# Collecting the experts' sums: the first batch added on VectorE, the second later and normalised on ScalarE, input halves taken from PSUM, the projection in two halves

## The reference

```
x = _layernorm(x + _L0_ffn_ref(x, ...), axis=-1)        # the experts' sums; x included
kva = x @ wkv_a                                        # 256 -> 64 + 64
ckv, k_pe = (kva[..., :LORA], kva[..., LORA:])
ckv = ckv * rsqrt(mean(ckv * ckv, -1) + EPS) * kv_norm_scale
k_pe = _rope(k_pe, cos, sin)
```

## Time and profile before

| | us |
|---|---|
| runs shown | 1349.69, 1347.46, 1347.89; median 1347.89 |
| the profiled execution | 1350.13, its span 1348.3 |
| TensorE busy | 1174.2 (87% of the span) |
| VectorE busy | 783.9 (58%) |
| ScalarE busy | 735.6 (55%) |
| GpSimd busy | 955.8 (71%) |
| collect phase, from its first load to the first attention instruction | 449.85 to 491.99 |

### The profile page before, as it was taken

One profiled execution on the slowest core, in us unless ns is written; L12 is line 12 of the kernel. 1 busy time (PEld: TensorE's weight loads), 2 busy tenths in 40 slices (PEclk: granted clock), 3 DMA queues, 4 the chain that ended last, 5 costly groups with the idle time before them and its releaser, 6 DMA issues. The chain is left out here.

```text
span 1348.3 us, 18919 instructions
## 1 busy us (share of the span) xinstructions
PE 1174.2 (87%) x5570; PEld 879.9 (65%) x5625; DVE 783.9 (58%) x1712; ACT 735.6 (55%) x1389; POOL 955.8 (71%) x700
## 2 busy tenths in 40 slices
PE   6982779999999248999999997869999999998797
PEld 4882645555555146777777775847777777777586
DVE  4478822222222375777777772857777777754566
ACT  3220223333333026888888887227888888885242
POOL 2023948888887546889988886648988899967454
PEclk9995879999999578999999999969999999998799
DMA  9439245555555600000000000000000000002001
GB/s 326 152 126 241 56 107 82 82 79 81 81 79 77 180 9 9 8 9 8 1 9 9 1 1 13 1 16 4 6 9 9 9 9 1 1 0 70 0 16 47
DMA packets 66512, 68.22 MB, mean 51 GB/s; under 512 B 15072, under 2 KB 59680, under 8 KB 66304
## 3 DMA queue, kind: packets, MB, share of 16 engines
q1 hardware_dynamic: 48336, 43.36, 10.9%
q0 software_dynamic: 15168, 20.72, 10.0%
q10 hardware_dynamic: 2928, 3.15, 0.7%
HBM read 46.10 MB, written 21.10 MB: 50 GB/s over the span
## 5 line engine op out<-in xcount | busy, mean ns | idle before, releaser
L1537 POOL TENSOR_TENSOR att_prob_lo<-att_prob,att_prob_hi 128x1024 fp32r<-128x1024 f32 (+1 forms) x160 | 348.2, 2181 | 78.6 <-ACT att_prob_hi L1460 78.4
L1360 PE MATMUL all_bank<-att_q_hl,sequence_k_hl 128*128 128x512 f32 (+1 forms) x960 | 259.0, 380 | 0.0
L1383 PE MATMUL all_bank<-att_prob_hi,sequence_v_hl 128*128 128x512 f32 (+1 forms) x640 | 188.8, 376 | 5.9 <-POOL att_prob_lo L1537 3.1
L1360 PEld LDWEIGHTS all_bank<-att_q_hl,sequence_k_hl 128*128 128x128 f32 x960 | 173.0, 192 | 28.9
L1343 PE MATMUL all_bank<-sequence_k_hl,att_q_hl 128*128 128x512 f32 (+3 forms) x384 | 171.2, 450 | 18.7 <-DVE att_peak L1585 11.7
L1453 ACT ACTIVATE att_prob<-all_bank 128x1024 f32<-128x1024 f32 (+1 forms) x160 | 149.9, 937 | 62.7 <-PE all_bank L1366 56.2
L1460 ACT CAST att_prob_hi<-att_prob 128x1024 fp32r<-128x1024 f32 (+1 forms) x160 | 154.2, 964 | 5.1
L917 PE MATMUL all_bank<-early_w_gu,moe_xgT 128*128 x316 | 148.8, 553 | 3.6 <-issue 2.5
L882 POOL DMA_INDIRECT sums<-moe_y,early_slot_far x79 | 125.4, 1588 | 36.4 <-issue 20.8
L1572 DVE TENSOR_TENSOR all_xT<-all_bank,sequence_cst_turned 32x512 f32<-32x512 f32 x128 | 88.7, 693 | 96.7 <-PE all_bank L1330 95.7
L1596 DVE RECIPROCAL att_rden<-att_den 128x128 f32<-128x128 f32 x124 | 116.3, 944 | 29.0 <-POOL late_oT L1532 29.0
(11 more groups left out here) (246 smaller groups left out, 2192.4 us busy)
## 6 DMA issues: line engine op xcount, KB each, us to landing
sequence_w_raw<-wqk_rows SPq DMA_DIRECT2D x16, 256.0 KB, 2.6
early_w_gu<-in_gate SPq DMA_DIRECT2D x16, 224.0 KB, 5.7
early_w_gu<-in_up SPq DMA_DIRECT2D x16, 224.0 KB, 5.8
early_w_down<-in_down SPq DMA_DIRECT2D x1, 3584.0 KB, 20.0
sums<-early_zero SPq DMA_DIRECT2D x18, 128.0 KB, 3.7
all_xT<-in_xT SPq DMA_DIRECT2D x4, 512.0 KB, 8.5
all_x_tok<-in_x SPq DMA_DIRECT2D x1, 2048.0 KB, 16.3
x_rows<-all_x_tok SPq DMA_DIRECT2D x4, 512.0 KB, 3.0
```

Source lines behind the costliest of these rows:

```text
L1360: nc.tensor.matmul(ps, k_hl[:, ks, j * P:(j + 1) * P], q_hl[n % 2][:, qs, :, i * BW + q0:(i + 1) * BW], start=g == 0, stop=False)
L1383: mm = nc.tensor.matmul(out, v_hl[:, vs, j, :], part[:, u % 3, half * WIDE:half * WIDE + 2 * w].rearrange("p (h m) -> p h m", h=2), start= ...
L1537: nc.gpsimd.tensor_tensor(prob_lo[:, u % 3, 0:w], prob[:, u % 2, 0:w], prob_hi[:, u % 3, 0:w].bitcast(F32), ALU.subtract).then_inc(lo_sb, 1)
```

## The change

GpSimd no longer adds groups 0 and 1; VectorE does, ahead of each group's statistics. GpSimd's adds of groups 2 and 3 wait until all of batch 0 is normalised. Groups 2 and 3 are normalised by ScalarE as Identity(rstd * z + shift), with shift = -mean * rstd made on GpSimd in two small instructions per group. The halves of batch 0's input are no longer made from `xT` in SBUF: ScalarE casts and VectorE subtracts each of the four PSUM banks that hold the transposed tiles (`x_high`, `x_low`), and TensorE may reuse a bank only after both. TensorE projects tiles 0 to 3 between its first two groups of transposes, tiles 4 to 7 behind the second, and puts `turn` ahead of the last group. On VectorE the query weights' halves, and the copies of the projection, move ahead of batch 1's statistics. In the output phase the copies of the projection are only called from another place, in the same order.

```diff
@@ -1068,9 +1068,9 @@
-    def project(self, pe):
+    def project(self, pe, tiles=range(QT)):
         pe.wait_ge(self.loaded, 32)
-        for t in range(QT):
+        for t in tiles:
...
     def highs(self, act):
         self.nc.scalar.copy(self.x_hl[:, 0], self.x_own).then_inc(self.x_sb, 1)
+        self.ones_high(act)
+
+    def ones_high(self, act):
         act.wait_ge(self.ones_sb, 1)
         self.nc.scalar.copy(self.v_hl[:, 0, :, LORA:P], self.ones[:]).then_inc(self.v_sb, 1)
 
@@ -1096,15 +1099,18 @@
             act.wait_ge(self.turn_mm, g + 1)
             self.nc.scalar.copy(self.k_hl[:, 0, g * WIDE:(g + 1) * WIDE], self.turn_ps[g]).then_inc(self.k_sb, 1)
 
+    def begin(self, dve):
+        self.step = Count(self.step_sb, dve)
+
+    def copy_raw(self, dve, g):
+        dve.wait_ge(self.raw_mm, g + 1)
+        self.nc.vector.tensor_copy(self.raw[:, g * self.GT:(g + 1) * self.GT, :],
+                                   self.raw_ps[g].rearrange("p (t n) -> p t n", n=P)).then_inc(self.raw_sb, 1)
+
     def finish_rows(self, dve):
-        v, step = self.nc.vector, Count(self.step_sb, dve)
-        self.step = step
+        v, step = self.nc.vector, self.step
         half = ROPE // 2
         raw, rows = self.raw, self.rows
-        for g in range(self.G):
-            dve.wait_ge(self.raw_mm, g + 1)
-            v.tensor_copy(raw[:, g * self.GT:(g + 1) * self.GT, :], self.raw_ps[g].rearrange("p (t n) -> p t n", n=P)
-                          ).then_inc(self.raw_sb, 1)
...
             @block.gpsimd
             def _(pool):
-                for g in range(G):
+                def add(g):
                     at = slice(g * GT, (g + 1) * GT)
                     pool.wait_ge(loaded[g], 32)
                     nc.gpsimd.tensor_tensor(z[:, at, :], z[:, at, :], odd[:, at, :], ALU.add).then_inc(z_sb, 1)
-                    if g:
-                        norm.deviations(pool, g - 1)
-                norm.deviations(pool, G - 1)
+
+                def shifts(g):
+                    at = slice(g * GT, (g + 1) * GT)
+                    nc.gpsimd.tensor_scalar(less_mean[:, at], norm.meanvar[:, at, 0], -1.0, None, ALU.mult
+                                            ).then_inc(less_sb, 1)
+                    pool.wait_ge(less_sb, g - OWN + 1)
+                    pool.wait_ge(norm.rstd_sb, g + 1)
+                    nc.gpsimd.tensor_tensor(shift[:, at], less_mean[:, at], norm.rstd[:, at], ALU.mult).then_inc(shift_sb, 1)
+
                 latent.make_ones(pool)
+                for g in range(OWN):
+                    norm.deviations(pool, g)
+                pool.wait_ge(norm.x_sb, OWN * GT)
+                for g in range(OWN, G):
+                    add(g)
+                for g in range(OWN, G):
+                    norm.deviations(pool, g)
+                    shifts(g)
                 latent.rms(pool)
-                for k in range(KC):
-                    latent.input_rest(pool, k)
 
             @block.vector
             def _(dve):
-                for g in range(G):
+                def add(g):
+                    at = slice(g * GT, (g + 1) * GT)
+                    dve.wait_ge(loaded[g], 32)
+                    nc.vector.tensor_tensor(z[:, at, :], z[:, at, :], odd[:, at, :], ALU.add).then_inc(z_sb, 1)
+
+                def statistics(g):
                     dve.wait_ge(z_sb, g + 1)
                     norm.statistics(dve, g)
-                    if g:
-                        norm.normalise(dve, g - 1)
-                norm.normalise(dve, G - 1)
+
+                def x_low(n):
+                    g, k = divmod(n, KC)
+                    at = slice(g * WIDE, (g + 1) * WIDE)
+                    dve.wait_ge(x_hi_sb, n + 1)
+                    nc.vector.tensor_tensor(x_hl[:, 1, k, at], bank[:, n % 4, :], x_hl[:, 0, k, at].bitcast(F32),
+                                            ALU.subtract).then_inc(x_lo_sb, 1)
+
+                latent.begin(dve)
+                add(0)
+                statistics(0)
+                add(1)
+                norm.normalise(dve, 0)
+                statistics(1)
+                norm.normalise(dve, 1)
+                latent.weights(dve)
+                x_low(0)
+                x_low(1)
+                latent.copy_raw(dve, 0)
+                statistics(2)
+                x_low(2)
+                x_low(3)
+                statistics(3)
+                latent.copy_raw(dve, 1)
                 latent.finish_rows(dve)
-                latent.weights(dve)
                 latent.key_rest(dve)
 
             @block.tensor
             def _(pe):
-                for g in range(G):
-                    if g == OWN:
-                        pe.wait_ge(xT_sb, OWN * KC)
-                        latent.project(pe)
+                def turn(g):
                     for k in range(KC):
                         n = g * KC + k
                         if n >= 4:
                             pe.wait_ge(xT_sb, n - 3)
+                            pe.wait_ge(x_lo_sb, min(n - 3, OWN * KC))
                         for i in range(GT):
                             t = g * GT + i
-                            pe.wait_ge(norm.x_sb, t + 1)
+                            if t < OWN * GT:
+                                pe.wait_ge(norm.x_sb, t + 1)
+                            else:
+                                pe.wait_ge(late_sb, t - OWN * GT + 1)
                             mm = nc.tensor.transpose(bank[:, n % 4, i * P:(i + 1) * P], x_tok[:, t, k * P:(k + 1) * P],
                                                      cst["ident"])
                         mm.then_inc(xT_mm, 1)
+
+                turn(0)
+                pe.wait_ge(xT_sb, KC)
+                latent.project(pe, range(GT))
+                turn(1)
+                pe.wait_ge(xT_sb, OWN * KC)
+                latent.project(pe, range(GT, QT))
+                turn(2)
                 latent.turn(pe)
+                turn(3)
 
             @block.scalar
             def _(act):
-                load(act, odd, sums[1])
-                for n in range(G * KC):
+                def copy_x(n):
                     g, k = divmod(n, KC)
                     act.wait_ge(xT_mm, n + 1)
                     nc.scalar.copy(xT[:, k, g * WIDE:(g + 1) * WIDE], bank[:, n % 4, :]).then_inc(xT_sb, 1)
-                act.wait_ge(xT_sb, OWN * KC)
-                latent.highs(act)
+
+                def x_high(n):
+                    g, k = divmod(n, KC)
+                    nc.scalar.copy(x_hl[:, 0, k, g * WIDE:(g + 1) * WIDE], bank[:, n % 4, :]).then_inc(x_hi_sb, 1)
+
+                def normalise(g):
+                    act.wait_ge(shift_sb, g - OWN + 1)
+                    for t in range(g * GT, (g + 1) * GT):
+                        nc.scalar.activation(x_tok[:, t, :], z[:, t, :], ACT.Identity, bias=shift[:, t:t + 1],
+                                             scale=norm.rstd[:, t:t + 1]).then_inc(late_sb, 1)
+
+                load(act, odd, sums[1])
+                for g in range(OWN):
+                    for k in range(KC):
+                        copy_x(g * KC + k)
+                    for k in range(KC):
+                        x_high(g * KC + k)
+                latent.ones_high(act)
+                normalise(2)
+                for k in range(KC):
+                    copy_x(2 * KC + k)
+                normalise(3)
                 latent.key_highs(act)
+                for k in range(KC):
+                    copy_x(3 * KC + k)
...
                 if latent:
+                    latent.begin(dve)
+                    for g in range(latent.G):
+                        latent.copy_raw(dve, g)
                     latent.finish_rows(dve)
```

11 lines of the change are left out of this document (7 added, 4 removed).

## The result

| | before | after |
|---|---|---|
| median of 22 runs | 1347.30 | 1340.21 |
| lowest, highest | 1336.95, 1349.84 | 1331.34, 1344.49 |
| profiled execution, span | 1350.13, 1348.3 | 1340.02, 1338.2 |
| mean granted clock in it | 0.932 | 0.936 |

The ratio is 0.9946, with a 95% interval of 0.9932 to 0.9959: faster by 7.1 us by the medians, where 5.3 were forecast.

What follows compares the result with a forecast made beforehand. No single engine bounds the kernel; in the edited stage before the attention, mostly VectorE's path. 1.5 + 4.1 - 0.25 = 5.35, say 5.3 us, from 1347.9 gives 1342.6; own range 1340.4 to 1344.0, 8 in 10 1340.2 to 1345.0.

Steps and rivals of the forecast that it cites:

- the way up to square: VectorE's sequence between the last expert and the attention: its square starts at 476.4 instead of 477.86, 1.5 us won.
- the attention starts with the same instructions, only earlier: Attention phases behind the edited stage: nothing changes but the starting moment, so no term in the sum.
- Unit and rows, 4.1 us: VectorE behind GpSimd's rrms: with GpSimd idle these take 1.5 us instead of 5.56, the largest term.
- Tail, 0.25 lost: From the rows' end to the stage's end: sixteen TensorE transposes and copies take 4.3 us against 4.05.
- GpSimd's shift, 0.3 for the product: Batch 3's shift on GpSimd ahead of rms: product taken as 0.3 us, costing nothing; at its upper bound 0.4 lost.
- ScalarE's normalising: Batch 1's eight normalisings on ScalarE: hidden up to about 0.55 us each; rival that they become the path, slower, 0.03.
- The rival that TensorE enters at the high clock: Attention's query matmuls: 16 transposes ahead raise the clock, first six take 1.3 us less, total 1341.3; chance 0.15.
- The base: Starting time from which the gain was subtracted: 1347.9, the median of the three runs shown.

Runs made afterwards that it cites:

- e3: Kernel before, with only the input's halves made from PSUM and no input_rest on GpSimd; phase 38.80 us against 42.18, profiled run 1344.86.
- e4: Kernel after, with the halves made from xT again and GpSimd's two input_rest back; phase 38.77 us against 36.18, profiled run 1344.74.
- e1: Kernel after, with turn(3) ahead of turn on TensorE and its copies ahead of the keys' casts; phase 35.34 us against 36.18, profiled run 1335.53.
- e14: Kernel after, with turn(3) ahead of turn, timed in 6 runs; phase 35.87 us, median 1336.25, ratio to before 0.9927.
- e13: Kernel after, unchanged, run a third time on another chip, 7 runs; phase 36.31 us, median 1337.17, ratio to before 0.9926.
- e15: Kernel after, with the query weights' cast on ScalarE, their subtraction on GpSimd, wkva and scale loaded early; 12 runs, median 1341.06, ratio to before 0.9953.
- e5: Kernel after, without GpSimd's wait ahead of its late adds; phase 39.22 us against 36.18, profiled run 1335.67.
- e9: Kernel after, unchanged, run again, 4 runs; phase 36.94 us, median 1336.27, ratio to before 0.9926.
- e6: Kernel after, with VectorE normalising batch 1 as well; phase 39.05 us against 36.18, profiled run 1336.67.

## Why the prediction was right in its steps and wrong in its size

Two steps of it failed. The term for the way up to square was mis-sized, 1.5 us where 2.28 were measured; and the sum had no term for TensorE's clock behind the phase ("the attention starts with the same instructions, only earlier"), where the medians hold at least 1.1 us more than the phase gives.

**Unit and rows, 4.1 us.** Right, and shown: 4.06, by e3 and e4 due to GpSimd's subtraction.

**Up to square, 1.5 us.** This is the term that was mis-sized: it measured 2.28. The order and the releasers were as forecast: adds of 1.23 on VectorE, projection released by the load of the scale and its first half 3.75 us long, the weights' subtraction stretched to 2.72, no wait between the normalisings and square. But each four normalisings take 1.38, not the 1.55 of the earlier trace rows. The timeline of the kernel before shows it too, and beside it, from GpSimd's timeline, what lay over the longer one:

```profile
471.21 1.35 DVE L478 TENSOR_SCALAR all_x_tok<-middle_z,collect_ln_meanvar,collect_ln_rstd 128x256 f32<-128x256 f32 x4
472.75 0.52 POOL L1061 MEMSET collect_ones<- 128x512 f32 x1
```

I had taken the longer one, which begins at 472.83, under this memset of GpSimd. In e3 the same four begin 0.40 us behind the memset's end and take 1.37:

```profile
469.90 0.52 POOL L1061 MEMSET collect_ones<- 128x512 f32 x1
470.82 1.37 DVE L478 TENSOR_SCALAR all_x_tok<-middle_z,collect_ln_meanvar,collect_ln_rstd 128x256 f32<-128x256 f32 x4
```

In the kernel after, the memset is long past (446.88). That and the relay around them brought the second four to an end at 15.87 us from the load (462.74 - 446.87), where 16.35 were forecast. The subtraction was 0.2 shorter than reckoned and the sequence behind it 0.14. The Trainium skill, "SBUF — State Buffer", section "Who interferes with whom", lets the second to issue be blocked wholly. The prediction reckoned by it as if both began together. But the subtraction began 0.29 us behind the add (463.12, 462.83), so by the rule it waits 2.33 - 0.29 and then runs its 0.69, 2.73 in all. The trace agrees, with 2.72. GpSimd's second add began at 465.25, beneath the subtraction, and took 2.81 instead of 2.33 (it is the second of the two in the row of 5.23 above); and x_low, with one input in PSUM, took 1.28 for two beneath that add, as the two of key_rest did in the earlier trace rows:

```profile
465.76 1.28 DVE L1225 TENSOR_TENSOR sequence_x_hl<-all_bank,sequence_x_hl 128x512 fp32r<-128x512 f32 x2
```

**Tail, 0.25 lost.** Measured 0.30 (from the rows' end, 477.85, to ScalarE's last copy, 482.20, 4.35 against 4.05); e1 shows that it is the order of turn and turn(3), and that the other order would have been 0.84 better (0.44 by e14 and e13).

**GpSimd's shift, 0.3 for the product.** It took 0.20, and rms was not held up. **ScalarE's normalising.** 0.52 each, just under the bound of 0.55 up to which it is hidden; not the path.

**The attention starts with the same instructions, only earlier.** True of the instructions, and wrong of their time. The rival that TensorE enters at the high clock, given 0.15, came in two of the kernel's three profiles and is worth 1.27. It is no sure gain of the change: in e13 the same code has the low entry. Beyond it the prediction knew nothing of the 7 us between executions of the same code; it allowed 1 us either way. At equal clock the two kernels differ as the phase does: four runs of before at 0.939 to 0.942 have a mean of 1341.4, nine of after 1336.7, 4.7 less (straight lines through the 31 runs of before and the 33 of after, time against clock, lie 4.7 apart at 0.933 and 5.3 at 0.940). And as 6 us of a phase that runs at 0.58 are gone, the mean clock rises by 6 x (0.936 - 0.58) / 1342 = 0.0016 by that alone, 1.3 us by the slope: together 6.0, an estimate that rests on few runs. The phase itself is 5.2 to 6.0 shorter in the three profiles of the kernel after (36.94, 36.31 and 36.18 against 42.18), so it fits. What the medians show above this goes with the mix of clocks: the 31 runs of before that have a clock on record beside the experiments have a mean of 0.933, the 33 of after 0.938. e14 kept that mix and e15, with a still shorter phase, lost it. What gives which clock stays open, and so does whether the mix would be the same after any other edit further up.

**The base.** The forecast stood on the median of three, 1347.89; that of 22 is 1347.30. Of the 2.4 us between 1342.6 and 1340.2 this is 0.6, the phase 0.7 (0.8 up to square, less a little in the tail), and 1.1 is what the medians hold above the phase, put down to the clock by the estimate above and not shown part by part.

## What to carry to other kernels

Cost an instruction from all its rows, not from one: four rows of the same four normalisings (3.15, 2.17, 1.35, 1.55) stood in one timeline, three of them beneath an add or a memset of GpSimd's, and the fourth was the right one. When GpSimd and VectorE both read SBUF, it pays to do the one's work from PSUM on the other, or to move one of the two in time; the first was 4.06 of the 6.00 here, the second (the hold-back) is worth 2.3 by e5 and e9. And where the clock moves between executions by more than the edit is worth, measure the edit by its own stretch from a fixed instruction, and the time by many runs; one run of the early-load version gave 1334.4, twelve a median of 1341.1. A single execution can differ in a race of hundredths as well as in its clock, so an experiment is compared with an execution that fell the same way.

## What was not expected of the hardware

A GpSimd instruction of four numbers a partition takes 1.04 us, and 2.11 when VectorE's add of 1.23 begins 0.03 us ahead of it; it takes 1.04 or 1.05 when it begins 0.01 to 0.13 ahead itself (e6, the kernel after). Four normalisings of VectorE take 1.38 us with GpSimd idle, 1.55 when a GpSimd memset of 0.52 begins 0.08 ahead, 3.15 beneath one GpSimd add and 5.44 beneath two. And the granted clock differs between executions of the same kernel by 0.930 to 0.948, which is 13 us of 1340.
